# Second attention: row tiles in shifted order within a head step, and the 128-row operations at four places a batch

## What is computed

```
h = _layernorm(x, ln_g, ln_b)
kv = h @ W_kv
qk, v = jnp.split(kv, 2, axis=-1)      # 16 heads of 8
scores = jnp.einsum('bhqd,bhkd->bhqk', qk, qk)
a1 = jax.nn.softmax(scores, axis=-1)
a1 = jnp.einsum('gh,bhqk->bgqk', W_x, a1)
o1 = jnp.einsum('bhij,bhjd->bhid', a1, v)
return o1 @ W_out
```

## Time and profile before

| | us |
|---|---|
| median of 3 runs | 1661.07 |
| lowest, highest | 1660.34, 1665.47 |
| profiled execution | 1660.28 |
| its span | 1658.4 |
| mean granted TensorE clock | 0.967 |

### The profile page before, as it was taken

How to read it: one execution, slowest core, us unless ns; L and a number is a source line. 1 busy time by engine, 2 the same in 40 slices (tenths; PEclk the granted TensorE clock), 3 DMA queues, 4 the chain that set the end, 5 groups by cost and what they waited for, 6 DMA issues and landing times. The chain is left out here.

```text
span 1658.4 us, 56350 instructions
## 1 busy us (share of the span) xinstructions
PE 1571.1 (95%) x17756; PEld 1120.3 (68%) x17756; DVE 1269.6 (77%) x3471; ACT 1062.7 (64%) x2468; POOL 967.8 (58%) x1129
## 2 busy tenths in 40 slices
PE   4999999999999889988999999999999999998998
PEld 3344444444444367765888888888888888887997
DVE  5778888888878479977777777777877777773666
ACT  0567777777777656763676666676676667774332
POOL 4445454544443045556877887778877788762222
PEclk7899999999999899997999999999999999999999
DMA  7333333333333100012222222222222222200111
GB/s 208 101 103 106 105 102 114 101 106 104 105 100 98 34 23 28 28 46 85 82 79 64 73 80 79 75 65 70 83 75 68 71 75 83 69 31 14 63 63 54
DMA packets 170167, 129.07 MB, mean 78 GB/s; under 512 B 13036, under 2 KB 143224, under 8 KB 170104
## 3 DMA queue, kind: packets, MB, share of 16 engines
q1 hardware_dynamic: 169136, 127.65, 24.9%
q10 hardware_dynamic: 968, 0.60, 0.1%
HBM read 60.56 MB, written 54.53 MB: 69 GB/s over the span
## 5 line engine op out<-in xcount | busy, mean ns | idle before, releaser
L817 DVE TENSOR_REDUCE shifts<-bank 128x2 bf16<-128x512 f32 x1024 | 693.2, 692 | 159.8 <-PE bank L972 146.0
L767 ACT ACTIVATE probs<-bank 128x512 f32<-128x512 f32 x1024 | 588.6, 594 | 156.6 <-PE bank L965 143.3
L911 PE MATMUL bank<-values,probs 64*128 64x129 f32 x8192 | 576.8, 279 | 0.7 <-DVE o_even L785 0.6
L911 PEld LDWEIGHTS bank<-values,probs 64*128 64x128 f32 x8192 | 508.7, 188 | 51.7 <-issue 26.8
L965 PE MATMUL bank<-q_stack,k_stack 49*128 49x256 bf16 x2048 | 384.8, 276 | 38.0 <-DMA q_stack<-shift_rows 27.9
L972 PE MATMUL bank<-k_stack,q_stack 48*128 48x256 bf16 x2048 | 388.7, 280 | 11.6 <-DMA q_stack<-score_parts 7.4
L593 POOL TENSOR_TENSOR values<-mix,v_in 128x1024 f32<-128x1024 f32 x128 | 301.3, 2364 | 3.0 <-ACT v_in L733 3.0
L965 PEld LDWEIGHTS bank<-q_stack,k_stack 49*128 49x128 bf16 x2048 | 145.2, 95 | 181.9 <-issue 76.7
L602 POOL TENSOR_TENSOR o_odd<-o_odd,scaled 128x256 f32<-128x256 f32 x224 | 162.9, 727 | 148.4 <-ACT scaled L697 148.4
L697 ACT ACTIVATE scaled<-bank,recips 128x128 f32<-128x128 f32 x448 | 139.2, 362 | 111.0 <-DVE recips L811 109.8
L902 PE MATMUL bank<-probs,values 128*32 128x256 f32 x2048 | 170.4, 406 | 0.0
(11 more groups left out here) (146 smaller groups left out, 2159.9 us busy)
## 6 DMA issues: line engine op xcount, KB each, us to landing
score_parts<-parts SPq DMA_DIRECT2D x128, 192.0 KB, 2.3
k_stack<-score_parts SPq DMA_DIRECT2D x256, 96.0 KB
q_stack<-score_parts SPq DMA_DIRECT2D x256, 96.0 KB
score_parts<-parts SPq DMA_DIRECT2D x128, 128.0 KB, 2.2
score_parts<-parts SPq DMA_DIRECT2D x128, 64.0 KB, 1.8
x_in_f<-x_all SPq DMA_DIRECT2D x64, 128.0 KB, 2.0
x_in<-in_L_attn_x SPq DMA_DIRECT2D x32, 128.0 KB, 3.1
q_stack<-shift_rows SPq DMA_DIRECT2D x256, 2.0 KB
```

Of the source, the lines that this page charges most:

```text
L767: act.activation(probs[:, s % RING, :, :].rearrange("p t n -> p (t n)"), s2[s % 2][:, :], ACT.Exp, scale=scale).then_inc(exp_done, 1)
L817: dve.tensor_reduce(shifts[:, :, hf, col], s1[s % 2][:, :].rearrange("p (t n) -> p t n", t=TILES), op=ALU.max, axis=AX.X, negate=True).the ...
L911: return pe.matmul(pv_bank(h)[:, q * (D + 1):(q + 1) * (D + 1)], probs[rows, h % RING, t, q * P:(q + 1) * P], values[b.odd][rows, t, h, :] ...
```

## The change

The change touches the second attention (`first` false); the code of the first is only moved to functions of its own.

- Within a step, TensorE's order is no longer scores, then lower and upper products in turn, but `rows_apart`: one lower product, the two score matmuls of row tile 1, then lower and upper products with the upper ones a product later, and the two score matmuls of row tile 0 at the end. At an odd step the second scores lie in tile 1 and the first scores in tile 0, at an even step the other way round. The wait for `half_done` stands ahead of the first upper product, those of the lower products ahead of the first lower one.
- The 128-row operations stand at four places: shifts and q at step 1 (q of batch i + 2, before i + 3 at step 15), shifts and ot at 9, out at 11, v (of batch i + 2) and xt at 13. v and the shifts have columns of their own in the shared bank. The shifts are padded with zeros to 128 columns.
- The first bf16 part is written by ScalarE from PSUM beside `exact` (`take_qk`, now at step 1), the second by ScalarE at step 4 (`second_part`); GpSimd keeps the two subtractions, the last at step 5 (`last_part`).
- ScalarE writes v_in at step 15 instead of 2, and the normed rows behind the exponential of step 15 instead of ahead of it.

```diff
-        self.shifts0 = 11 if first else 12
-        self.v = 14 if first else 2
+        self.shifts0 = 11 if first else 9
+        self.v, self.v_ahead = (14, 1) if first else (13, 2)
         self.xt = 0 if first else 13
-        self.q = 3 if first else 15
+        self.q, self.q_ahead = (3, 3) if first else (1, 2)
...
-        self.ot = 11 if first else 8
-        self.out = 13 if first else 10
+        self.ot = 11 if first else 9
+        self.out = 13 if first else 11
...
+                if s == 5 and on(slots.split):
+                    last_part(i.plus(slots.split))
...
+            if not first:
+                pool.wait_ge(part0_ready, times(b, 0, n))
+                wait(pool, part1_ready, times(b, -1, n))
+                pool.tensor_tensor(rest[:, :, :], exact[:, :, :], parts[:, 0, :, :], op=ALU.subtract).then_inc(rest_ready, 1)
+                return
...
             act.activation(exact[:, 0, :], m1[:, 0:TOK], ACT.Copy).then_inc(qk_taken, 1)
+            wait(act, parts_written, times(b, -1, n) * (32 * len(RUNS)))
+            act.activation(parts[:, 0, 0, :], m1[:, 0:TOK], ACT.Copy).then_inc(part0_ready, 1)
...
+        def second_part(b):
+
+            act.wait_ge(rest_ready, times(b, 0, n))
+            act.activation(parts[:, 1, 0, :], rest[:, 0, :], ACT.Copy).then_inc(part1_ready, 1)
 
         def step(i, on):
             for s in range(HEADS):
+                if not first and s == slots.q and on(slots.q_ahead):
+                    take_qk(i.plus(slots.q_ahead))
+                if not first and s == 4 and on(slots.q_ahead):
+                    second_part(i.plus(slots.q_ahead))
                 if s == slots.shifts1 and on(0):
                     shift_rows_out(i, 1)
...
+        def rows_apart(i, on, s):
...
+            def score(row_tile, t):
+                if s % 2 == row_tile:
+                    if on(0):
+                        second_score(i, s, t)
+                elif on(1):
+                    first_score(i.plus(1), s, t)
+
+
+            lower(0)
+            score(1, 0)
+            score(1, 1)
+            lower(1)
+            upper(0)
+            lower(2)
+            upper(1)
+            lower(3)
+            upper(2)
+            score(0, 0)
+            upper(3)
+            score(0, 1)
...
+        def others_of_second(i, on, s):
+
+            if s == 1 and on(0):
+                pe.wait_ge(shift_rows_ready, i.number() * 2 + 1)
+                wait(pe, v_taken, times(i, 1, n))
+                wait(pe, xt_ready, times(i, 2, n))
+                shifts_turned(i, 1)
+            if s == slots.q and on(slots.q_ahead):
+                b = i.plus(slots.q_ahead)
+                pe.wait_ge(xt_ready, times(i, slots.q_ahead, n))
+                wait(pe, v_taken, times(i, 1, n))
+                pe.matmul(m1[:, 0:TOK], core.w1_qk[:, :], x_t[b.odd][:, :], start=True, stop=True).then_inc(qk_in_psum, 1)
...
+            if s == slots.v and (on(slots.v_ahead) or on(3)):
+                wait(pe, y_ready, times(i, -1, n))
```

More of the change, by code:

```diff
@@ L35 @@
 BESIDE = 2
+SHIFTS_AT = 2 * TOK
 class Slots:
@@ L768, in step @@
                                    scale=scale).then_inc(exp_done, 1)
+                if not first and s == slots.norm and on(-1):
+                    norm(i.plus(-1))
         return step
@@ L928, in products @@
[L928 to L946, removed]
@@ new lines, in upper_product, with second_score @@
+        def upper_product(b, h, k):
+            if k == 0:
+                pe.wait_ge(half_done, b.number() * HEADS + (h + 1))
+            product = half_of_products(b, h, 1, k)
+            if k == TILES * TILES - 1:
+                product.then_inc(pv_done, 1)
+        def second_score(b, s, t):
+            if t == 0:
+                if s % half_heads == 0:
+                    pe.wait_ge(shifted[s // half_heads], b.number() * 32 + 32)
+                wait(pe, exp_done, b.number() * HEADS + (s - 1))
+            rows = stack_rows(s % 2, HEAD_ROWS + 1)
+            score = pe.matmul(s2[s % 2][:, t * TOK:(t + 1) * TOK], core.k_stack[b.odd][rows, s // 2, t * P:(t + 1) * P],
+                              core.q_stack[b.odd][rows, s // 2, :], start=True, stop=True)
+            if t == TILES - 1:
+                score.then_inc(s_in_psum, 1)
@@ L977, in step @@
         def step(i, on):
             for s in range(HEADS):
[L979 to L1008, removed]
-                        wait(pe, qk_taken, times(i, 3, n) * 2)
-                        wait(pe, shift_rows_ready, times(i, 0, n) * 2)
-                    else:
-                        wait(pe, qk_taken, times(i, 3, n) * 2 - 1)
-                        wait(pe, y_ready, times(i, -2, n))
-                    for t in range(TILES):
-                        for g in range(2):
-                            last = pe.transpose((m0, m1)[k][:, (2 * t + g) * P:(2 * t + g + 1) * P],
-                                                heads_t[b.odd][:, 2 * k + g, t * P:(t + 1) * P], core.ident[:, :])
-                    last.then_inc(heads_in_psum, 1)
@@ L1052, in step @@
-                if s == slots.xt and on(3):
-                    b = i.plus(3)
-                    pe.wait_ge(x_loaded[b.odd], (b.half + 1) * 16)
-                    wait(pe, y_ready, times(i, -2 if first else -1, n))
-                    wait(pe, qk_taken, times(i, 2, n) * sides)
-                    if not first and on(1):
-                        pe.wait_ge(shift_rows_ready, i.plus(1).number() * 2 + 1)
-                    for t in range(TILES):
-                        last = pe.transpose(m1[:, t * P:(t + 1) * P], x_in[b.odd][:, t, :], core.ident[:, :])
-                    last.then_inc(xt_in_psum, 1)
```

271 lines of the change are left out of this document (171 added, 100 removed).

## The result

| | before | after |
|---|---|---|
| median, us (4 runs each) | 1660.7 | 1707.64 |
| lowest to highest | 1658.87 to 1665.47 | 1703.49 to 1714.39 |
| span of the profiled run | 1658.4 | 1703.7 |
| ratio, 95% interval | 1 | 1.0282 (1.024 to 1.0324) |

A forecast was written before the change was run, and what follows sets the result against it. TensorE's stream was taken as the bound: steps 17.9, places 3.25 and waits 3.0 make 24.2 us a batch against 23.2, so some 31 batches add 31 us to 1661, giving 1692 us, range 1635 to 1732.

The forecast's parts named there:

- Part 1: TensorE's order within a step: the `half_done` wait is hidden, steps take 1.12 us, a gain of 1.5 a batch.
- rival (c): Matmuls start strictly in program order, so a step takes 1.21 us instead of 1.12; 1719 us in all, chance 0.08.
- Part 2: Gathering TensorE's 128-row operations at four places: together 3.25 us a batch, a gain of 0.55.
- Part 3: Casts: GpSimd loses two of 0.73 us, ScalarE gets two copies of 0.27; the later parts stay covered, 3 us to spare.
- Part 4: New TensorE waits, mostly for product banks that VectorE and ScalarE free late: eight chains, 3.0 us a batch.
- the sum of the waits: All new waits of TensorE in a batch added up: 3.0 us.
- Step 0 in the same way 0.21: Wait ahead of step 0, worked out like step 15's chain of reciprocal, sums and scaling: 0.21 us.
- TensorE's busy share: Sign to look for in the profile after the change: a fall from 99% to about 90%.
- rival (d): An unlisted wait, such as late DMAs or GpSimd's norm factors, adds one to two us: 1725 to 1760, chance 0.06.
- Rival (a): Faster: waits add up to less than the order's gain of 2.0 us; 1645 with waits of 1.5, chance 0.21.
- step 3's L0: First lower product of step 3: VectorE's chain from step 1 takes 2.91 us against 2.83, a wait of 0.08.
- the 0.59 of the q copies: Wait at step 2 for head 13, whose scaling stands behind q's two copies on ScalarE: 1.71 against 1.12 us.

The follow-up runs named there:

- e2: Changed kernel with the old order within a step, keeping the four places and the casts on ScalarE: 1667.55 us, 1.003 of the kernel before.
- e8: Changed kernel with both casts back on GpSimd: 1711.55 us, 1.0268 of the kernel before.
- e6: Changed kernel with VectorE's maximum a step later and ScalarE's scaling ahead of the copies in every odd step: 1650.16 us, 0.9924 of the kernel before.
- e9: Changed kernel with ScalarE's v_in copy at step 15 moved behind the scaling of head 11: 1701.67 us, 1.0234 of the kernel before.
- e3: Changed kernel with VectorE's maximum queued a step later, behind that step's reciprocal and sum: 1686.32 us, 1.0115 of the kernel before.
- e4: Changed kernel with ScalarE's scaling of head 13 ahead of q's copies at step 1: 1711.49 us, 1.0281 of the kernel before.
- e1: Kernel before with only the shifted order within a step, its seven places and GpSimd casts kept: 1677.69 us, 1.0071 of the kernel before.

## Why the prediction was right, and where it was short

**Part 1** held. Steps with nothing in their way (4 and 11 in the table below) take 1.12. That 1.12 is also where rival (c) would have shown, which has 1.21 for every step. A score of the one tile starts between the two passes of a product of the other: the last of the fourteen product records from 1216.22 starts at 1216.94 (1216.22 + 0.99 - 0.27), the score follows at 1217.00 and the product's second pass at 1217.05, although the program has that score ahead of that product. The trace does not agree here with what the prediction quoted from the Trainium skill (TensorE: Matmul & The Clock Gate, The mechanism), that matmuls start in program order.

**Part 2** held. Shifts and q take 1211.31 to 1212.01, so with the way in of 0.20 and less one slot 0.70 + 0.20 - 0.11 = 0.79, forecast 0.85. In e2 the four places take 3.17, forecast 3.25. Inside the place q starts 0.12 behind the shifts. The shifts' weights have 128 columns here, so by the rule of the Trainium skill (TensorEngine Tiling (Array Packing), Key Properties) that the prediction quoted, nothing drains between them; the trace agrees, and no run here gathered them with 8 columns.

**Part 3** held: e8 shows that the casts' place does not matter to the time, and in the changed kernel's list of waits from 780 to 1470 us no matmul and no weight load waits for a DMA.

**Part 4** decided the result, and its mechanism is what the runs show. In the table a step counts from the start of its first pair of scores to that of the next; "forecast" is 1.12 plus the terms that the prediction gave for the step and for the place behind it.

| step | forecast | after | e6 |
|---|---|---|---|
| 1, 2, 3 | 1.71, 1.20, 1.12 | 1.70, 1.18, 1.20 | 1.12, 1.18, 1.26 |
| 4, 5, 6, 7 (ahead of 8) | 5.35 together | 1.12, 1.19, 1.26, 1.79 | 1.12, 1.18, 1.12, 1.56 |
| 8 with place 9 | 1.74 | 1.67 | 1.77 |
| 9 (ahead of 10) | 1.45 | 1.55 | 1.12 |
| 10 with out | 1.85 | 1.86 | 1.94 |
| 11 | 1.12 | 1.12 | 1.12 |
| 12 with v and xt | 2.25 | 2.23 | 2.16 |
| 13 (ahead of 14) | 1.67 | 1.78 | 1.12 |
| 14, 15 (ahead of 15, 0) | 2.73 together | 1.24, 1.83 | 1.17, 1.67 |
| 0 with shifts and q | 1.97 | 1.92 | 2.00 |

**The term that was mis-sized** is the sum of the waits: 3.0 forecast, and about 3.5 measured (24.66 - 17.9 - 3.25). Most of the difference lies ahead of step 0: steps 13 to 15 are 4.85, forecast 4.40. "Step 0 in the same way 0.21" took step 15's chain over and missed an instruction: the change moves v_in's copy to step 15, ahead of head 11's scaling. ScalarE's timeline, with nothing idle between them:

```profile
1208.43 0.60 ACT L787 ACTIVATE probs<-bank 128x512 f32<-128x512 f32 x1 [1.15 <-PE bank L975]
1208.93 0.38 ACT L757 ACTIVATE v_in<-bank 128x256 f32<-128x256 f32 x1
1209.19 0.63 ACT L710 ACTIVATE scaled<-bank,recips 128x128 f32<-128x128 f32 x2
```

The reciprocal of head 11 was there at 1208.90 (1208.74 + 0.16):

```profile
1208.74 0.16 DVE L833 RECIPROCAL recips<-bank 128x2 f32<-128x2 f32 x1
```

So the scaling started 0.27 late, and L0 of step 0 followed at 1209.87. e9 took the copy out of that spot and won 0.18. The remaining 0.3 of 0.5 is spread: the waits of steps 10 and 14 are 0.1 longer each than worked out (in one batch their weight loads start 0.12 and 0.11 behind the end of the scaling, where those of steps 0, 2 and 8 start 0.05 to 0.06 behind it and 0.05 was put), and no run takes the last 0.1 apart. The places, 0.1 below their forecast, hide as much of the error. That the time missed by 16 us and the batch by 0.45 (31 times 0.45 is 14) is the same error.

**A sign that was missed.** TensorE's busy share was to fall to about 90% and fell to 95%. The forecast took every wait for idle time. A matmul's record lasts 0.27 or more where the next one of its tile can start 0.11 behind it, so records cover part of each gap: ahead of step 8 the matmuls show 0.29 of idle time, the weight loads 0.56. And rival (d)'s one to two us more a batch are 1723 to 1754 us, not 1725 to 1760, which changes nothing.

**Rival (a)** was wrong for a reason that e3 to e6 give: half the waits can be had back, but only by changing the order on VectorE and ScalarE, where the change left VectorE's as it was and put copies ahead of ScalarE's scalings. The 1645 that rival (a) worked out for waits of 1.5 is about what e6 takes (1650), with 22.63 - 17.9 - 3.25 = 1.5 of waits left. Its premise, that VectorE has time to spare, is true and did not help: VectorE waited for one score while the reciprocal and sum that TensorE needed stood behind it in its own order.

**The spot of steps 1 and 2** was right in sum, but I read it wrongly when I made e4. The prediction's own terms hold what e4 found: step 3's L0 comes 2.91 behind step 1 by VectorE's chain, whatever step 2 does, so the 0.59 of the q copies is no gain when they go; it only moves behind the next L0. A list of waits in which each is counted on top of the last one is right as a sum and wrong as a price list for edits.

**Left open**: in e6, steps 7 and 15 still wait 0.4 to 0.5. Its timelines ahead of step 8 show an order once more, on both engines. The rows are those of the last upper products of head 3, of the maximum and head 3's reciprocal, and of the exponential of step 6 and head 3's scaling:

```profile
1204.51 0.36 PE L943 MATMUL bank<-values,probs 64*128 64x129 f32 x2
...
1204.47 0.69 DVE L839 TENSOR_REDUCE shifts<-bank 128x2 bf16<-128x512 f32 x1
1205.07 0.16 DVE L833 RECIPROCAL recips<-bank 128x2 f32<-128x2 f32 x1
...
1204.93 0.60 ACT L787 ACTIVATE probs<-bank 128x512 f32<-128x512 f32 x1 [0.69 <-PE bank L981]
1205.43 0.62 ACT L710 ACTIVATE scaled<-bank,recips 128x128 f32<-128x128 f32 x2
```

The first of the two product records is the last upper one, the second, at 1204.60, is step 7's L0. The upper products end at 1204.78 (1204.51 + 0.27), and the reciprocal comes 0.29 later, behind a maximum. It is there at 1205.23, and the scaling starts 0.20 later, behind an exponential that had waited for the second scores at the end of step 6. Step 8's L0 comes at 1206.10 and was due at 1205.72 (1204.60 + 1.12). Had both started at once, an estimate with these rows' durations, 0.07 from the products' end to the reciprocal (the 1.28 + 0.07 of the prediction), 0.20 for it and 0.05 to the weights puts L0 at 1204.78 + 0.07 + 0.20 + 0.62 + 0.05 = 1205.72, in time; so the three banks may be enough, and the late exponential is what e6 did not move. Neither that nor a fourth bank was tried.

## What to carry to other kernels

A denser order on the bounding engine pays only as far as the engines that free its buffers keep step: for each first use of a buffer, write out the chain that frees it, with every instruction queued ahead on each engine, including the small ones that the change moves there, and keep the second longest chain too, since an edit that removes the longest may win nothing. When such a wait appears, look first at the order of the engine that releases it: an instruction that waits for a late input should stand behind those whose input is there (e3; the exponential of e6 is the next one). And an interruption of the bounding engine is not pure cost: it covers chains, so its removal and a denser order have to be costed together (e1, e2 and the change).

## What the runs showed of the hardware that I had not expected

128-row operations of different kinds follow each other within a slot inside a place, also where bf16 matmuls are followed by fp32 ones (1211.31 to 1211.43, 0.12 for the two transposes of the shifts); the prediction had taken this from a row of a single kind. And restarts of the stream differ: at step 8 the first score starts 0.08 behind the L0 that waited (1221.34, 1221.42), at step 0 it starts 0.22 behind (1209.87, 1210.09). What holds it back at step 0 was not tried; the 0.1 that no run explains may be there.

```profile
1209.87 0.49 PE L937 MATMUL bank<-values,probs 64*128 64x129 f32 x2 [0.21 <-ACT scaled L710]
1210.09 0.28 PE L989 MATMUL bank<-k_stack,q_stack 48*128 48x256 bf16 x1
```
